# Local attention in a decoder kernel: scores of two steps issued as four 64x64 products at a time, projections first on TensorE, value and head copies on VectorE

## The reference, cut to what matters

```python
qkv = x @ Wqkv                       # x: 4 x 512 x 128, 16 heads of 64
q, k = l2norm(q) * qs, l2norm(k) * ksc
q = q * cos * scale + rotate_half(q) * sin * scale
k = k * cos / scale + rotate_half(k) * sin / scale
sim = einsum('bhwie,bhwje->bhwij', bq, bk2) * 8.0   # a window of 32 and the one before it
attn = softmax(where(mask, -max, sim), -1)
out = einsum('bhwij,bhwje->bhwie', attn, bv2)
return out @ Wo
```

## Time and profile before

| | |
|---|---|
| median of 3 runs | 6191.35 us (6187.56 to 6226.92) |
| the profiled execution | 6185.92 us |
| its span | 6184.0 us |
| mean granted clock of TensorE | 0.867 |
| busy: PE, DVE, ACT, POOL | 81%, 52%, 48%, 31% |
| calls of `local_attention` | 6, of 342.8 us for the first (1349.4 to 1692.2) |

### The profile page before, as it was taken

How to read it: one execution, slowest core, us unless ns; L and a number is a source line. 1 busy time by engine, 2 the same in 40 slices (tenths; PEclk the granted TensorE clock), 3 DMA queues, 4 the chain that set the end, 5 groups by cost and what they waited for, 6 DMA issues and landing times. The chain is left out here.

```text
span 6184.0 us, 108311 instructions
## 1 busy us (share of the span) xinstructions
PE 5032.6 (81%) x39346; PEld 3240.5 (52%) x39346; DVE 3189.3 (52%) x6332; ACT 2957.8 (48%) x8829; POOL 1901.8 (31%) x2082
## 2 busy tenths in 40 slices
PE   3998598978878878878788788778989944787888
PEld 2664255756636546546456456458886632223433
DVE  5551354556546446455356366358875544562433
ACT  2442244547647657556467477355534412352421
POOL 0230000347637457367277187001112300000000
PEclk6999799999989989899899799776669966895888
DMA  1000000001101111111111011000000000000000
GB/s 48 2 1 4 19 10 16 1 14 39 47 19 41 40 29 36 35 34 35 31 39 41 25 40 41 32 1 1 1 1 5 1 3 4 10 4 29 4 0 7
DMA packets 34520, 122.70 MB, mean 20 GB/s; under 512 B 8484, under 2 KB 9512, under 8 KB 32424
## 3 DMA queue, kind: packets, MB, share of 16 engines
q1 hardware_dynamic: 33960, 115.42, 6.9%
HBM read 36.43 MB, written 1.05 MB: 6 GB/s over the span
## 5 line engine op out<-in xcount | busy, mean ns | idle before, releaser
L640 POOL MEMSET norm_eps<- 128x1 f32 x16 | 1.6, 99 | 1905.7 <-POOLq L116 1847.2
L2087 POOL TENSOR_TENSOR local_rot<-local_raw,local_cos 128x512 f32<-128x512 f32 x384 | 488.1, 1271 | 303.5 <-DVE local_raw L2131 303.5
L2090 POOL TENSOR_TENSOR local_other<-local_raw,local_sin 128x256 f32<-128x256 f32 x768 | 557.6, 726 | 60.2
L2029 ACT ACTIVATE ps<-ps,local_negmax 128x96 f32<-128x96 f32 x1536 | 489.2, 322 | 37.2 <-DVE local_negmax L2110 36.9
L1952 PE MATMUL ps<-arena,local_xs 128*128 128x512 f32 x768 | 447.4, 667 | 71.8 <-ACT local_xs L2009 52.0
L2093 POOL TENSOR_TENSOR local_rot<-local_rot,local_other 128x512 f32<-128x512 f32 x384 | 487.4, 1269 | 30.1
L2024 ACT ACTIVATE local_squares<-ps 128x512 f32<-128x512 f32 x384 | 230.8, 601 | 508.2 <-PE ps L1952 507.8
L2117 DVE TENSOR_REDUCE local_norm<-local_squares 128x8 f32<-128x512 f32 x384 | 263.2, 685 | 282.4 <-ACT local_squares L2024 282.4
L1940 PE MATMUL ps<-local_K,local_Q 64*64 64x96 f32 x6144 | 337.0, 249 | 0.0
L2029 ACT ACTIVATION_READ_ACCUMULATOR ps<-ps,local_negmax 128x1 f32 x1536 | 331.0, 215 | 0.0
L2519 PE MATMUL ps<-ssm_BC,const 32*128 32x40 f32 (+1 forms) x3584 | 297.8, 373 | 26.4 <-PEq L116 22.0
(11 more groups left out here) (499 smaller groups left out, 11465.9 us busy)
## 6 DMA issues: line engine op xcount, KB each, us to landing
local_V_span<-local_V SPq DMA_DIRECT2D x96, 384.0 KB, 4.0
local_V_span<-local_V SPq DMA_DIRECT2D x96, 256.0 KB, 3.5
arena<-in_L1f_a SPq DMA_DIRECT2D x7, 2176.0 KB, 8.2
local_V_span<-local_V SPq DMA_DIRECT2D x72, 128.0 KB, 2.3
arena<-in_L3f SPq DMA_DIRECT2D x1, 3460.0 KB, 11.6
arena<-in_L1f_f SPq DMA_DIRECT2D x6, 537.5 KB, 4.0
arena<-in_L0f SPq DMA_DIRECT2D x1, 2824.5 KB, 9.8
arena<-in_L0x SPq DMA_DIRECT2D x1, 2049.5 KB, 9.0
```

The lines of the kernel that those rows point to most:

```text
L2029: nc.scalar.activation(scores, scores, ACT.Exp, bias=m.negmax[:, s % 2, u:u + 1], accum_out=m.total[:, s % 2, u:u + 1])\
L2087: link(nc.gpsimd.tensor_tensor(rot, raw, m.cos[:, t, a * DH:(a + 1) * DH].unsqueeze(1) .broadcast_to([P, 8, DH]), ALU.mult))
L2090: link(nc.gpsimd.tensor_tensor(other[:, :, lo:lo + HALF], raw[:, :, HALF - lo:DH - lo], m.sin[:, t, a * DH + lo:a * DH + lo + HALF].unsque ...
```

## The change

- Scores: PE issues the scores of steps `s` and `s + 1` together, in even `s`. After two masks come, for each of four `u` and two halves of rows `h`, the products of both steps `i`. The output rows are exchanged for the second step (`rows_of`), so that four neighbouring products use the four combinations of row half and column half. The values read `pts` by the same exchange. `scores_ready` counts pairs; the pair waits for all four units of its tile (`flip_read`) and for `probs` of `s - 2`.
- PE's order in a step: projection, scores (even steps), turned `rot`, value projection, turned `probs`, values, output projection. The output projection comes in step `4 * tile + 9` instead of `4 * tile + 7`.
- ACT's order: squares, copy to `Q` or `K`, Ln and Exp, exponentials, `pts`. The copies to `V` and `oT` are gone from ACT.
- DVE's order: token sum, sums of squares, negated maximum, `raw`, copy to `V`, head copy to `oT`, reciprocal and `probs`. The clamp is gone: Ln has a bias of 1e-35 (a constant column `tiny`), and `raw` is made by `scalar_tensor_tensor` with a minimum of 1e12 on the inverse.
- `LEAD` is 7 instead of 6, and there are two more steps at the end.

```diff
     G = UNITS * TILES
-    LEAD, TURN_LAG = 6, 3
-    STEPS = range(-LEAD, G + 5)
+    LEAD, TURN_LAG = 7, 3
+    STEPS = range(-LEAD, G + 7)
...
+    def turning_out(s):
+
+        tile = s // 4 - 2
+        return tile if s % 4 == 1 and 0 <= tile < TILES else None
...
-        if s % 4 == 3 and s >= 4:
-            uses.append(("out", s // 4 - 1))
+        if turning_out(s) is not None:
+            uses.append(("out", turning_out(s)))
...
+    def rows_of(h, half):
+
+        o = h if half == 0 else 1 - h
+        return slice(DH * o, DH * o + DH)
...
-                if 0 <= s < G:
-                    tile, half_span, half = place(s)
-                    pe.wait_ge(flip_read, flips_until(4 * tile + 2 * half + 1))
...
-                g = s - 1
-                if 0 <= g < G:
-                    pe.wait_ge(probs_ready, g + 1)
-                    if g >= 1:
-                        pe.wait_ge(pts_ready, g)
+                if 0 <= s < G and s % 2 == 0:
+                    tile, half_span, _ = place(s)
+                    pe.wait_ge(flip_read, 4 * tile + 2 * 1 + 2)
+                    if s >= 2:
+                        pe.wait_ge(probs_ready, s - 1)
+                    first = tile % QT * TILE + SPAN_Q * half_span
+                    edge = int(tile % QT == 0 and half_span == 0)
+                    for i in range(2):
+                        nc.tensor.matmul(SC[(s + i) % 3][:, 0:UNITS * SPAN], m.unit[:, :],
+                                         m.bands[:, edge, :, :].rearrange("p u k -> p (u k)"), start=True, stop=False)
                     for u in range(UNITS):
-                        mm = nc.tensor.transpose(PT[0:SPAN, u * P:(u + 1) * P], m.probs[:, g % 2, u, :], core.ident)
-                    mm.then_inc(turned, 1)
+                        for h in range(2):
+                            for i in range(2):
+                                c = UNITS * i + u
+                                rows = slice(DH * h, DH * h + DH)
+                                mm = nc.tensor.matmul(SC[(s + i) % 3][rows_of(h, i), u * SPAN:(u + 1) * SPAN],
+                                                      m.Q[rows, tile % 2, c, SPAN_Q * half_span:SPAN_Q * (half_span + 1)],
+                                                      m.K[rows, c, first:first + SPAN], start=False,
+                                                      stop=(u == UNITS - 1))
+                    mm.then_inc(scores_ready, 1)
...
-                        pe.wait_ge(flip_read, flips_until(n - 1))
+                        pe.wait_ge(flip_read, n)
...
+                g = s - 1
+                if 0 <= g < G:
+                    pe.wait_ge(probs_ready, g + 1)
+                    if g >= 1:
+                        pe.wait_ge(pts_ready, g)
+                    for u in range(UNITS):
+                        mm = nc.tensor.transpose(PT[0:SPAN, u * P:(u + 1) * P], m.probs[:, g % 2, u, :], core.ident)
+                    mm.then_inc(turned, 1)
...
-                                                  m.pts[:, g % 3, u, h * SPAN_Q:(h + 1) * SPAN_Q],
-                                                  start=True, stop=True)
+                                                  m.pts[:, g % 3, u, rows_of(h, half)], start=True, stop=True)
                     mm.then_inc(heads_done, 1)
-                if s % 4 == 3 and s >= 4:
-                    tile = s // 4 - 1
+                tile = turning_out(s)
+                if tile is not None:
                     pe.wait_ge(out_read, 2 * (tile + 1))
...
             for s in STEPS:
-                g = s - 3
-                if 0 <= g < G and g % 2 == 1:
-                    tile, half_span, _ = place(g)
-                    act.wait_ge(heads_done, g + 1)
-                    if tile >= 2:
-                        act.wait_ge(projected, tile - 1)
-                    nc.scalar.copy(m.oT[:, tile % 2, :, SPAN_Q * half_span:SPAN_Q * (half_span + 1)],
-                                   OUT[:, :].rearrange("p (c q) -> p c q", q=SPAN_Q)).then_inc(out_read, 1)
                 n = s + LEAD
                 if n < G:
                     act.wait_ge(qk_ready, n + 1)
                     if n >= 2:
                         act.wait_ge(summed, n - 1)
                     nc.scalar.activation(m.squares[:, n % 2, :], bank("qk", n)[:, :], ACT.Square).then_inc(squared, 1)
+                n = s + LEAD - TURN_LAG
+                if 0 <= n < G:
+                    tile, i = divmod(n, 4)
+                    c = 4 * (i // 2)
+                    act.wait_ge(flipped, n + 1)
+                    if i % 2 == 0:
+                        if tile >= 2:
+                            act.wait_ge(scores_ready, 2 * (tile - 1))
+                        nc.scalar.mul(m.Q[:, tile % 2, c:c + 4, :], TURN[:, :].rearrange("p (c q) -> p c q", c=4),
+                                      QK_SCALE).then_inc(flip_read, 1)
+                    else:
+                        t = tile % QT
+                        if tile >= QT:
...
+                n = s + LEAD
+                if n < G:
+                    act.wait_ge(summed, n + 1)
+                    if n >= 4:
+                        act.wait_ge(scaled, n - 3)
+                    nc.scalar.activation(m.log[:, n % 4, :], m.norm[:, n % 4, :], ACT.Ln, bias=m.tiny[:, 0:1])\
+                      .then_inc(log_ready, 1)
+                    act.wait_ge(log_ready, n + 1)
+                    nc.scalar.activation(m.inverse[:, n % 4, :], m.log[:, n % 4, :], ACT.Exp, scale=-0.5)\
+                      .then_inc(inverted, 1)
...
-                n = s + LEAD
-                if n < G:
-                    act.wait_ge(summed, n + 1)
-                    if n >= 4:
-                        act.wait_ge(scaled, n - 3)
-                    nc.scalar.activation(m.log[:, n % 4, :], m.norm[:, n % 4, :], ACT.Ln).then_inc(log_ready, 1)
-                    act.wait_ge(log_ready, n + 1)
-                    nc.scalar.activation(m.inverse[:, n % 4, :], m.log[:, n % 4, :], ACT.Exp, scale=-0.5)\
-                      .then_inc(inverted, 1)
-                n = s + LEAD - TURN_LAG
...
-                n = s + LEAD
-                if n < G and n % 4 in (1, 2):
-                    tile, i = divmod(n, 4)
-                    v = 2 * tile + i - 1
-                    act.wait_ge(v_ready, v + 1)
...
-                if s % 4 == 0 and s >= 8:
-                    tile = s // 4 - 2
+                sc = SC[s % 3][:, 0:UNITS * SPAN].rearrange("p (u k) -> p u k", k=SPAN)
+                tile = turning_out(s - 1)
+                if tile is not None:
                     place_x = core.tokens[:, tile // QT, PAD + tile % QT * TILE:PAD + (tile % QT + 1) * TILE]
                     dve.wait_ge(projected, tile + 1)
                     nc.vector.tensor_tensor(place_x, bank("out", tile)[:, 0:TILE], place_x, ALU.add)\
                       .then_inc(x_done, 1)
-                if 0 <= s < G:
-                    sc = SC[s % 3][:, 0:UNITS * SPAN].rearrange("p (u k) -> p u k", k=SPAN)
-                    dve.wait_ge(scores_ready, s + 1)
-                    nc.vector.tensor_reduce(m.negmax[:, s % 2, :], sc, AX_X, ALU.max, negate=True)\
-                      .then_inc(max_ready, 1)
                 n = s + LEAD
                 if n < G:
                     dve.wait_ge(squared, n + 1)
                     if n >= 4:
                         dve.wait_ge(inverted, n - 3)
-                    link(nc.vector.tensor_reduce(m.norm[:, n % 4, :], heads(m.squares[:, n % 2, :]), AX_X, ALU.add))
-                    nc.vector.tensor_scalar(m.norm[:, n % 4, :], m.norm[:, n % 4, :], 1e-24, None, ALU.max)\
+                    nc.vector.tensor_reduce(m.norm[:, n % 4, :], heads(m.squares[:, n % 2, :]), AX_X, ALU.add)\
                       .then_inc(summed, 1)
+                if 0 <= s < G:
+                    dve.wait_ge(scores_ready, s // 2 + 1)
+                    nc.vector.tensor_reduce(m.negmax[:, s % 2, :], sc, AX_X, ALU.max, negate=True)\
+                      .then_inc(max_ready, 1)
+                if n < G:
+                    if n >= 4:
+                        dve.wait_ge(rotated, n - 3)
+                    dve.wait_ge(inverted, n + 1)
+                    nc.vector.scalar_tensor_tensor(out=heads(m.raw[:, n % 4, :]),
+                                                   in0=m.inverse[:, n % 4, :].unsqueeze(2).broadcast_to([P, 8, DH]),
+                                                   scalar=1e12, in1=heads(bank("qk", n)[:, :]), op0=ALU.min, op1=ALU.mult)\
+                      .then_inc(scaled, 1)
...
+                if n < G and n % 4 in (1, 2):
+                    tile, i = divmod(n, 4)
+                    v = 2 * tile + i - 1
+                    dve.wait_ge(v_ready, v + 1)
+                    if tile >= 1:
+                        dve.wait_ge(spans_loaded[(tile - 1) % 2], dmas_until(tile - 1))
+                    if tile >= 2:
+                        dve.wait_ge(spans_loaded[tile % 2], dmas_until(tile - 2))
```

(9 more changed lines are left out.)

48 lines of the change are left out of this document (5 added, 43 removed).

## The result

| | before | changed |
|---|---|---|
| median of the runs | 6188.72 us (6185.15 to 6226.92, 5 runs) | 6466.64 us (6457.45 to 6506.09, 5 runs) |
| ratio, 95% interval | | 1.0448 [1.0404, 1.0493] |
| span of the profiled execution | 6184.0 us | 6494.1 us |
| mean granted clock | 0.867 | 0.826 |

The kernel became slower by 4.5%, 278 us. The prediction was 6212 us, no change that could be told, with a range up to 6330; it was 255 us short. The six layers of local attention last 387.0 us each in the changed kernel, on average, and 340.8 before; six times the difference is 277 us. The two profiled executions differ by 310 us: the other 34 lie behind the six layers (2334.9 and 2300.9 us), where the two programs are the same.

What follows compares the result with a forecast made beforehand. PE's work plus two head-copy waits were to make a tile 20.74 us against 20.43; tiles +3.7, start +2.0, run-out -2.3 gave +3.4 us a layer, +20 for six, 6206, plus 5.4 for the median: 6212 us, range 6110 to 6330.

Steps and rivals of the forecast that it cites:

- The scores: PE's masks and scores: four products run together, so a pair of steps takes 1.24 us instead of 2.14.
- The new wait: PE's values in every even step wait for DVE's head copy to `oT`, about 2.2 us each.
- The chain that leads to it: Slots added up through a tile, from projection and scores to head copy and values: four steps, 20.74 us against 20.43.
- an item that the text had named: Ln's bias and `raw` by `scalar_tensor_tensor`: taken at nothing; at 0.05 us each, 0.4 us a tile or 34 us in all.
- the clock still 1.00: Sign that the forecast is right: granted clock stays 1.00 in a tile near 20.7 us.
- PE busy below 80%: Sign that the forecast is right: PE's busy share in a tile near 20.7 us.
- The start: First projection to step 8: first scores need all four units turned, so the layer's start is 2.0 us longer.
- The run-out: Step 56 to the end: no projections, four pairs of scores, 34.3 us against 36.6, so 2.3 us shorter.
- The first: Rival: PE's wait for the head copy is short, a tile takes 17.55 us, 5963 us in all; chance 0.12.
- The second: Rival: only two score products run together, 0.66 us more a pair, tile 22.06 us, 6323 us; chance 0.14.
- The third: Rival: the chains are shorter than added up by 1 us a tile, 84 us, 6128 us; chance 0.10.
- The fourth: Rival: `V` copy behind the loads or DVE late by 0.7 us a tile, 59 us, 6271 us; chance 0.14.

Runs made afterwards that it cites:

- head copy behind the maximum: Changed kernel with VectorE's head copy moved between the negated maximum and the raw product: 6025.17 us, ratio 0.9739 against the kernel before.
- the kernel with the copy first: Changed kernel with VectorE's head copy moved from the end of its step to the beginning: 6012.82 us, ratio 0.9731 against the kernel before.
- the run with the same halves: Kernel with the head copy first, both steps of a pair using the same array halves, so products run two at a time: 6156.73 us, ratio 0.9939.

## Why the prediction was wrong

**What held.** The scores: 1.24 us a pair, predicted 1.24, and four products do run together. The rule that weighed against it, in the Trainium skill's page "TensorEngine Tiling (Array Packing)", section "Restrictions and Gotchas", is not borne out here: products of both row halves in one bank finish 32 in 0.89 us, and only when all use the same quarters do they take 1.59. The new wait: found in the place, for the copy, and of about the size given ("about 2.2 us each", measured 2.16 and 1.90). The chain that leads to it, step by step in a tile at full clock:

| step | predicted | measured at clock 1.00 | measured where the clock fell |
|---|---|---|---|
| 0 | 5.95 | 6.07 | 6.12 |
| 1 | 4.41 | 4.44 | 6.01 |
| 2 | 6.55 | 6.57 | 6.57 |
| 3 | 3.83 | 3.90 | 5.09 |
| tile | 20.74 | 20.98 | 23.79 |

0.24 us a tile is the sum's own error, 2.9 us over twelve tiles. It has the size of four longer Ln (each takes 0.30 us where the earlier trace rows has 0.23; it has a bias from memory now), an item that the text had named, with 0.05 us, and set to nothing. But that this is the cause isn't shown: steps 0 and 2 hold the same chain, and one is 0.12 us over its sum and the other 0.02.

**The step that failed** is the last sentence of the prediction's working: "Long idle of PE could also lower the granted clock; I count nothing for it, since the start holds such gaps." With it went "the clock still 1.00" (and "PE busy below 80%", which is 82% in the middle; in the tile at full clock it is 79%). Cut as the prediction cut it, the mean of the six layers is:

| stretch of a layer | before | predicted | changed | head copy behind the maximum |
|---|---|---|---|---|
| first projection to step 8 | 59.1 | 61.1 | 64.1 | 57.6 |
| twelve tiles, steps 8 to 55 | 245.1 | 248.8 | 281.4 | 212.6 |
| step 56 to the end | 36.6 | 34.3 | 41.5 | 38.9 |
| layer | 340.8 | 344.2 | 387.0 | 309.1 |

A layer is 42.8 us above the sum. The clock in the twelve tiles is the largest part: 281.4 us against 251.8, which is twelve of the changed kernel's own tiles at full clock, so 30 us a layer and 178 of the 255 us by which the forecast was short. The sum's own error in the tile is 17 more. The rest is in the two ends, which were each mis-sized too. The start is 3 us above its sum, 18 us in all; single steps of it are off by up to 2.2 us (in the second layer step 1 takes 4.0 us for 6.2, step 6 takes 8.3 for 6.6 and step 7 takes 5.9 for 3.8) and partly cancel, which is luck. The run-out was forecast 2.3 us shorter and is 4.9 longer, 43 us in all. Its clock was 1.00 before and is 0.87 in most layers now; with the head copy behind the maximum it is 0.91, and the run-out is still 4.6 us above the sum. How much of the two ends is the clock and how much the chains was not separated.

```profile
1837.03:1900.66 63.63, 47.27 (x354) 24.75 (x354) 36.67 (x67) 37.08 (x131) 55.78 (x58) 0.88 0.15 36
1900.66:2182.51 281.85, 232.11 (x2308) 152.82 (x2304) 152.44 (x299) 161.70 (x622) 190.96 (x192) 0.87 0.14 34
2182.51:2223.92 41.41, 32.17 (x414) 26.09 (x414) 17.12 (x39) 19.34 (x85) 7.98 (x8) 0.88 0.08 21
```

The reason given for counting nothing, that the start holds such gaps, is true of the trace before, and it doesn't carry the conclusion. The start of the first layer before, cut in two, and two of its waits:

```profile
1349.40:1362.80 13.40, 9.61 (x10) 2.85 (x10) 7.80 (x12) 6.65 (x14) 8.26 (x9) 0.50 0.14 42
1362.80:1410.50 47.70, 38.28 (x352) 24.17 (x353) 31.59 (x58) 33.67 (x126) 45.03 (x46) 1.00 0.19 48
```

```profile
1367.89 0.63 PE L1969 MATMUL ps<-const,local_rot 128*128 128x128 f32 x4 [1.60 <-ACT local_Q L2056]
...
1371.24 0.63 PE L1969 MATMUL ps<-const,local_rot 128*128 128x128 f32 x4 [1.87 <-ACT local_K L2062]
```

The 0.89 of the earlier trace rows is all from the first 13 us, at half clock, and TensorE had stood still for 10.37 us before the first projection. Behind the waits of 1.60 and 1.87 us the clock stayed at 1.00. So the trace before had gaps of nearly the new size that cost no clock, but it had no loop with two waits of about 2 us in every tile, and it couldn't say what such a loop does. A rival for it was missing, though its price could be had from the same trace: a projection at half clock takes 2.08 us (1358.89 in the first layer) where the earlier trace rows has 1.12. Putting the 0.89 of the earlier trace rows on PE's 16.4 us of work a tile would have given 18.4, 2.0 us more a tile, 146 us in all and 6358 us, beyond the range that was given; but that clock came from another cause, so coming near would have been luck. That the waits come in every tile was in the text and was not followed further. The Trainium skill's page "TensorE: Matmul & The Clock Gate", section "HAM oscillation — how this bites in real kernels", describes such a loop, in which each wait sends the array back to its lower clock; the waits of its example are longer than the ones here. By that account the trace agrees for most tiles, and the tile at 1984 us, with the same two waits at 1.00, shows that it is not so each time.

**The rivals.** The first ("The head copy does not bind", 17.55 us a tile, 5963 us, chance 0.12) described the kernel with the copy first: 17.71 and 6012.82. Its tile was right within 0.16 us, its time 50 us too low, and it was wrong for this kernel, where the copy does bind. The second (two at a time, 22.06 us a tile) was wrong in its cause; its price of 0.66 us a pair is 0.70 by the run with the same halves. The third (chains shorter by 1 us a tile) was wrong: at full clock the tile is 0.24 us longer than its sum. The fourth (V copy or DMA late) had next to no part: VectorE's V copies waited 7.1 us for the loads in the whole kernel.

**The range.** It was made from errors of the sum and from rivals that each changed one term at a full clock. None of them let the clock itself move, so its upper end of 6330 was the second rival's and held nothing for the case that came.

## What to carry to other kernels

A copy that frees a buffer belongs in its engine's order before whatever waits for the step at hand: moving one copy of 0.68 us (two of them a tile) from the end of VectorE's step to its start turned 4.5% slower into 2.7% faster, with the same work on every engine. When a change takes work from TensorE and leaves waits of some microseconds in a loop that ran at full clock, give the clock a rival of its own, with the price of the same products at half clock from the same trace, and treat it as a switch, not as a price per wait. A few such gaps elsewhere that left the clock alone, like those of the start here, don't show that a loop of them will. To tell whether the clock is the cause, put useless products into the wait: if the kernel gets faster, it is.
